# Scatters without batch waits, a reordered first and last batch, and a shorter tail in an mLSTM and mixture-of-experts block

## The reference

```python
xn = layernorm(x)                                # over the 128 features
# s: attention of 4 heads of 32 features, per batch
q, k, v = headwise products of xn with 4x4 blocks of wq, wk, wv
ig, fg  = three times xn through wi, wf, plus bi, bf
log_D   = cumulative log_sigmoid(fg), lower triangle, plus ig
D       = exp(log_D - row_max(log_D))
C       = (q @ k.T / sqrt(32)) * D
h       = (C / (max(|row_sum(C)|, exp(-row_max)) + 1e-8)) @ v
s       = layernorm(h, per head) * (1 + ln_w)
# g: mixture of 8 experts, each token goes to one
top1 = argmax(softmax(xn @ router_w + router_b))
for i in range(8):
    a, b = split(xn @ w1[i] + b1[i])             # 512 and 512
    y = (a * sigmoid(b)) @ w2[i] + b2[i]         # kept for tokens with top1 == i
g = silu(y of the token's expert)
out = x + s * g
```

## Time and profile before

| | us |
|---|---|
| time, median of 3 (range) | 235.09 (234.85 to 235.75) |
| the profiled execution's own time | 235.47 |
| its span, first to last instruction | 233.7 |
| PE busy | 217.2 |
| DVE busy | 162.4 |
| ACT busy | 140.3 |
| POOL busy | 92.6 |

### The profile page before, as it was taken

One profiled execution on the slowest core, in us unless ns is written; L12 is line 12 of the kernel. 1 busy time (PEld: TensorE's weight loads), 2 busy tenths in 40 slices (PEclk: granted clock), 3 DMA queues, 4 the chain that ended last, 5 costly groups with the idle time before them and its releaser, 6 DMA issues.

```text
span 233.7 us, 6082 instructions
## 1 busy us (share of the span) xinstructions
PE 217.2 (93%) x1824; PEld 173.1 (74%) x1834; DVE 162.4 (69%) x491; ACT 140.3 (60%) x326; POOL 92.6 (40%) x130
## 2 busy tenths in 40 slices
PE   8998989678899889999999999999999999998994
PEld 6787654234545454569999999999999999996541
DVE  5998699507467658755877987798779967963170
ACT  2398758456767676877556655665566555552044
POOL 5667930756566563000333333333433333335100
PEclk9999999976999999999999999999999999999999
DMA  6999999930179111400077021011101001000498
GB/s 180 328 363 418 337 205 210 209 111 34 49 202 327 35 48 44 129 3 28 18 223 255 14 67 57 23 57 56 47 28 52 22 26 35 17 22 13 110 341 267
DMA packets 23617, 29.26 MB, mean 125 GB/s; under 512 B 3319, under 2 KB 18687, under 8 KB 23585
## 3 DMA queue, kind: packets, MB, share of 16 engines
q1 hardware_dynamic: 18994, 20.42, 26.5%
q0 software_dynamic: 3424, 8.36, 14.5%
q10 hardware_dynamic: 1168, 0.10, 0.4%
HBM read 19.99 MB, written 9.34 MB: 126 GB/s over the span
## 4 chain that ended last, share of the span: by engine, by line
PE 73%; DVE 13%; issue 5%; ACT 2%; another core or an unknown queue 2%; DMA 2%; POOL 0%; DVEq 0%; SPq 0%; ACTq 0%
PE bank L1213 15%; PE bank L1222 15%; PE head_bank L1213 15%; PE head_bank L1171 5%; PE bank L1183 4%; DVE cm L876 4%; PE bank L1161 3%; DVE stats L711 2%; PE bank L1199 2%; PE head_bank L1141 2%; PE bank L1285 2%; DMA x_sb<-in_L_attn_x 2%; PE bank L1288 1%; PE head_bank L1285 1%
## 5 line engine op out<-in xcount | busy, mean ns | idle before, releaser
L450 POOL DMA_INDIRECT y_tokens<-ffn,idx x39 | 38.6, 991 | 88.1 <-DVE ffn L1004 87.5
L876 DVE TENSOR_TENSOR cm<-dm,head_bank 128x1024 f32<-128x1024 f32 (+1 forms) x32 | 29.1, 951 | 23.7 <-PE head_bank L1171 8.5
L444 POOL DMA_INDIRECT xs_sorted<-xn,pos x32 | 31.1, 973 | 28.0 <-PE head_bank L1171 10.5
L1222 PE MATMUL bank<-w_sb,dm 128*128 x312 | 41.3, 275 | 0.1
L1213 PE MATMUL bank<-xsT,wc 128*128 128x128 f32 x320 | 39.0, 275 | 0.0
L1222 PEld LDWEIGHTS bank<-w_sb,dm 128*128 128x128 f32 x312 | 38.0, 192 | 0.3 <-issue 0.3
L1213 PEld LDWEIGHTS bank<-xsT,wc 128*128 128x128 f32 x320 | 37.3, 192 | 0.0
L1213 PE MATMUL head_bank<-xsT,wc 128*128 128x128 f32 x304 | 37.0, 275 | 0.0
L1213 PEld LDWEIGHTS head_bank<-xsT,wc 128*128 128x128 f32 x304 | 35.5, 192 | 0.0
L586 ACT ACTIVATE wc<-w_sb 128x512 f32 x39 | 24.6, 630 | 14.4 <-issue 14.3
L565 ACT ACTIVATE dm<-bank 128x512 f32<-128x512 f32 x48 | 27.0, 597 | 8.1 <-PE bank L1161 7.5
(11 more groups left out here) (192 smaller groups left out, 345.5 us busy)
## 6 DMA issues: line engine op xcount, KB each, us to landing
x_sb<-in_L_attn_x SPq DMA_DIRECT2D x16, 256.0 KB, 5.1
w_sb<-in_L_ffn_w SPq DMA_DIRECT2D x8, 512.0 KB, 8.9
w_sb<-negated_rows POOLq DMA_DIRECT2D x8, 508.0 KB
xs_sb<-xs_sorted SPq DMA_DIRECT2D x13, 192.0 KB
xs_sorted<-b_sb SPq DMA_DIRECT2D x1, 2048.0 KB, 11.1
w_sb<-y_tokens SPq DMA_DIRECT2D x8, 256.0 KB, 4.4
out_x<-w_sb SPq DMA_DIRECT2D x8, 256.0 KB, 2.5
y_tokens<-ffn,idx POOLq DMA_INDIRECT x39, 2.3
```

Source lines behind the costliest of these rows:

```text
L444: pool.indirect_dma_start(xs_dram, bass.IndirectOffsetOnAxis(ap=pos[:, t:t + 1], axis=0), xn[:, t, :], None).then_inc(s_scat, 16)
L450: pool.indirect_dma_start(y_dram, bass.IndirectOffsetOnAxis(ap=idx[:, j:j + 1], axis=0), ys_sb[:, j // CH % 2, j % CH, :], None, bounds_ch ...
L876: dve.tensor_tensor(cm[:, b % 2, :, m0:m1, :], dm[:, b % 2, :, m0:m1, :], head_bank[:, :, m0 * P:m1 * P].rearrange("p h (m t) -> p h m t", ...
L1222: last = pe.matmul(bank[6 + j % 2][:, 0:D], uT[:, j % 2, c, :], w2_sb[:, bass.ds(e * (HC * D) + c * D, D)], start=(c == 0), stop=(c == HC ...
```

## The change

- GpSimd: the table `SCAT_AT` and the waits for it are gone. The scatters are issued one after the other once `pos` is there.
- VectorE, batch 0: the first step of `positions()` stays ahead; the other steps and the rows of decay 2 stand behind the weighing of batch 0.
- Batch 14: its token rows (TensorE) stand behind the hidden layer of block 0 in iteration 15, and their copy (ScalarE) behind the gate of block 0.
- Last blocks: ScalarE takes the output's sigmoid ahead of the gate for j = 38. VectorE does the silu ahead of the product and the bias for j = 38 and of the bias for j = 39.
- TensorE, tail: the warming before the last x-addition is gone.

```diff
@@ -55,7 +55,6 @@
     TP = T // NPC
     NSTEPS = 25
     SQUARES_AT = {1: (0, 1), 8: (2,), 9: (3,), 16: (4,), 17: (5,), 24: (6,), 25: (7,)}
-    SCAT_AT = [t * 13 // T for t in range(T)]
     GT = 8
     EPS_LN = 1e-5
     EPS_N = 1e-8
@@ -439,8 +438,6 @@
             pool.wait_ge(s_fill, 32)
             pool.wait_ge(s_pos, 1)
             for t in range(T):
-                if SCAT_AT[t] != (SCAT_AT[t - 1] if t else 0):
-                    pool.wait_ge(s_sc, SCAT_AT[t])
                 pool.indirect_dma_start(xs_dram, bass.IndirectOffsetOnAxis(ap=pos[:, t:t + 1], axis=0),
                                         xn[:, t, :], None).then_inc(s_scat, 16)
 
@@ -614,6 +611,12 @@
                 act.activation(sg[:, j % 2, :, :].rearrange("p c t -> p (c t)"), bank[2 * (j % 2) + 1][:, :],
                                ACT.Sigmoid).then_inc(s_th, 1)
 
+            def sigmoid(j):
+                act.wait_ge(s_yb, j + 1)
+                if j >= 2:
+                    act.wait_ge(s_ye, j - 1)
+                act.activation(sy[:, j % 2, :], yb[:, j % 2, :], ACT.Sigmoid).then_inc(s_sy, 1)
+
             decay(0, 0)
             decay(0, 1)
             evac_q(6)
@@ -628,6 +631,7 @@
                 if b == B - 1:
                     act.wait_ge(s_cm, 2 * (B - 1))
                     gate(0)
+                    outputs(b - 1)
                 if b + 2 < B:
                     decay(b + 2, 0)
                 if b == B - 2:
@@ -636,7 +640,7 @@
                 if b + 2 < B:
                     decay(b + 2, 1)
                     decay(b + 2, 2)
-                if b + 1 < B:
+                if b + 2 < B:
                     outputs(b)
                 if b == 5:
                     act.wait_ge(s_seld, 1)
@@ -659,15 +663,14 @@
                     evac_xs(j + 1)
                 if 2 <= j < NBLK - 1:
                     copy_w(j + 1)
+                if j == NBLK - 1:
+                    sigmoid(j - 2)
                 if 1 <= j < NBLK:
                     gate(j)
                 if j == 1:
                     outputs(B - 1)
-                if j >= 2:
-                    act.wait_ge(s_yb, j - 1)
-                    if j >= 4:
-                        act.wait_ge(s_ye, j - 3)
-                    act.activation(sy[:, j % 2, :], yb[:, j % 2, :], ACT.Sigmoid).then_inc(s_sy, 1)
+                if j >= 2 and j != NBLK - 1:
+                    sigmoid(j - 2)
                 for i in SQUARES_AT.get(j, ()):
                     squares(i)
 
@@ -889,12 +892,15 @@
 
             def attention():
                 blocks = experts_of_blocks()
-                for place in positions():
-                    link(place)
+                places = positions()
+                link(next(places))
                 dve.tensor_scalar(left[:, 1, :], sel[:, 0, :], lmask[:, 0, 1:2], lmask[:, 1, 1:2], ALU.mult, ALU.add).then_inc(s_lf1, 1)
-                left_rows(2)
                 for b in range(B):
                     weigh(b)
+                    if b == 0:
+                        for place in places:
+                            link(place)
+                        left_rows(2)
                     if b == 0:
                         dve.wait_ge(s_sel, 2)
                         dve.wait_ge(s_seld, 1)
@@ -1016,6 +1022,8 @@
                     if j >= 2:
                         copy_w(j + 1)
                         step(normals)
+                if j >= NBLK - 1:
+                    silu(j - 2)
                 if 1 <= j < NBLK:
                     product(j)
                     if j == 1:
@@ -1026,7 +1034,7 @@
                     token_index(j // CH)
                 if 1 <= j <= NBLK:
                     add_bias(j - 1)
-                if j >= 2:
+                if 2 <= j < NBLK - 1:
                     silu(j - 2)
                     step(normals)
             while step(normals):
@@ -1245,6 +1253,7 @@
                     pe.wait_ge(s_xone, 1)
                     pe.wait_ge(s_dm, 3 * B)
                     hidden(0)
+                    token_rows(b - 1)
                 if b + 2 < B:
                     log_decay(b + 2, 0)
                 if b == B - 2:
@@ -1280,8 +1289,6 @@
             pe.wait_ge(s_xr, 16 * NPC)
             pe.wait_ge(s_yb, NBLK)
             for g in range(NPC):
-                if g == NPC - 1:
-                    keep_warm(6, g)
                 pe.matmul(bank[g][:, :], ident[:, :], x_sb[:, g * TP:(g + 1) * TP, :], start=True, stop=False)
             for g in range(NPC):
                 pe.wait_ge(s_prod, g + 1)
```

## The result

| | before | after |
|---|---|---|
| time, median of 4 (range) | 235.42 (234.85 to 237.16) | 261.27 (259.74 to 262.58) |
| the profiled execution's own time | 235.47 | 261.54 |
| its span | 233.7 | 259.7 |
| mean granted clock of TensorE | 0.985 | 0.921 |
| weighing of batch 15 starts | 101.02 | 127.83 |

The ratio is 1.1082, with a 95% interval of 1.0996 to 1.1168. The forecast was 239.0 with a range of 232 to 247. Its sign was right; its size was off by 22 us, and the time lies outside the range.

The account below looks back on a forecast made before the run. The prediction took the kernel as bound nearly always by TensorE working or being kept from working. +6.2 - 0.5 - 1.6 = +4.1 on 235.47 gave 239.6, 239.2 as a median, rounded to 239; range 232 to 247.

Parts of the forecast that it names:

- The mechanism: Attention batches: while scatters go back to back, what waits on TensorE is released late, later the longer the stream is.
- only a third scatter costs: Rival, attention batches: a third scatter costs, stream length adds nothing; 235.6 us, or 232.7 at 4.65 throughout; chance 0.25.
- the stream costs nothing: Rival, attention batches: a continuous stream costs nothing after batch 2, batches at 3.2 us; 225.8 us; chance 0.15.
- the pace P: Time per attention batch inside the unpaced scatter stream: taken as 6.07 us, batch 15 weighed 6.2 us later; chance 0.45.
- as bad as its worst batch: Rival, attention batches: pace near 8.84 us beside the stream; 246.3 us, up to 249; chance 0.15.
- a fall of the clock: Part of the worst-pace rival: TensorE's granted clock falls once more, some 3 us, bringing 246.3 up to 249.
- The last batch: Batch 14's token rows moved behind the first expert block's hidden layer fill a TensorE idle: -0.5 us, between 0 and -0.5.
- The last silus: End of expert stage: earlier silus let the last scatter start at 215.3 instead of 216.23, -0.95 us for the reloads.
- The tail as a whole: Last silus and removed warming together: -1.95 us by the rows, taken as -1.6, between -1.0 and -1.95.
- The Trainium skill's rule: Attention batches: engines never wait on anyone, engine and DMA ports cannot contend; stream would cost nothing; prediction said trace disagrees.

Follow-up runs that it names:

- e2_nowait: The kernel before with only the scatters' batch waits removed, held-up series: 261.39 us, ratio 1.1117.
- e1_waits: The changed kernel with the scatters' batch waits put back, quiet series: 221.26 us, ratio 0.9911.
- h2_small: The kernel before with only the edits of last batch, last silus and warming, quiet series: 222.08 us, ratio 0.9943.
- r1_after: The changed kernel again, unaltered, in a second, held-up series: 261.82 us, ratio 1.1130.
- r3_waits: The changed kernel with the scatters' batch waits put back, run again in a held-up series: 237.73 us, ratio 1.0118.
- g2_narrow: The changed kernel with back-to-back scatters moving only 32 of 128 columns, held-up series: 262.49 us, one execution.
- g1_close: The changed kernel with a 96-column memset ahead of each scatter, starts 1.44 us apart, no batch waits, held-up series: 249.02 us, ratio 1.0584.
- f2: The changed kernel with a GpSimd memset ahead of each scatter, starts 1.58 us apart, no batch waits, held-up series: 231.98 us, one execution.
- f3: The changed kernel with plain, unsorted DMAs from GpSimd's queue in place of the 32 indirect scatters, held-up series: 222.91 us, one execution.
- e6: The changed kernel with plain, unsorted DMAs from SP's queue in place of the 32 indirect scatters, held-up series: 220.99 us, one execution.
- r2_before: The kernel before once more, for its trace in the second, held-up series: 237.84 us, one execution.
- f1_two: The changed kernel with waits allowing two scatters per batch, held-up series: 238.48 us, ratio 1.0124.

## Why the prediction was wrong in size

**The mechanism was read rightly, for the held-up kind.** While scatters are issued back to back, what waits on TensorE is released late, and later the longer the stream is. This came true. The scatters run 1.27 us apart from 42.60 to 82.17, as forecast (42.4 to 81.8). With the waits removed from before and nothing else, the loss is there. The rival in which only a third scatter costs (232.7 to 235.6) fell with e2_nowait, and the one in which the stream costs nothing (225.8) with it. In a quiet series that last one is what happens: e1_waits and h2_small have the dense stream and batches of 3.2 us. No row of the kernel before could show that there are two kinds, and the sign came out right because the result was taken in the kind in which the prediction's trace was.

**The step that failed is the pace P.** The text put it as "it can't be below 3.20 and the worst seen is 8.84", took 6.07, and gave +6.2 us. Measured is 127.83 - 101.02 = +26.8. The stream's passage from batch 1 to its end was to be 6.7 batches; it was less than two. The 6.07 was the mean of two unlike batches, 3.30 us (40.09 to 43.39, while the first scatters went out) and 8.84; after has 3.45 and 8.63 there, and then the stop. Both 6.07 and 8.84 were used as a pace that 32 scatters would hold. But the earlier trace rows had releases 3.47 (44.32 to 47.79) and 2.63 us behind the result after a few scatters, where the earlier trace rows had 1.31 after three. The text says "later the longer the stream is" and then bounds by the worst of the shortest stream. A delay that grows with the stream has no upper bound in a burst of eight; the bound was the whole stream: no batch passes until it ends. That is batch 1 at 83.8 and 14 batches at 3.20 behind it, 128.6 for batch 15. The measured 127.83 lies beside it, and so do r1_after (128.8 by this rule, 128.45 measured) and e2_nowait (127.0, 126.68). This rule was made after the result, and it fits in part by luck: batch 2 did pass, at 51.26, the release came 5.8 us behind the last scatter instead of 2.0, and the twelve behind it took 39.84 us, 3.32 each. The rival "as bad as its worst batch" (246 to 249) had the same flaw. Its upper end counts 3 us for a fall of the clock, for which it shows no row; the two batches at and behind the lower level took 1.5 us more in sum than at 3.20 each (3.81 and 4.08). The rival of the third scatter rests on six alternating intervals from batch 5 on; the three before them, from 52.23 to 64.36, take 3.87, 4.41 and 3.85 us and fit neither of its two paces.

**What the delay follows.** From the last scatter of a burst to the release behind it: 1.9 us after three (67.08 to 68.99), and 5.8 after 32 (82.17 to 87.97). In between lie 2.5 after the eight of before (49.69 to 52.23) and 2.7 after the ten of r3_waits (55.61 to 58.28); the other streams of 32 at 1.27 us have 5.6 (r1_after, g2_narrow) and 6.9 (e2_nowait). The plain reading is a backlog: each indirect scatter leaves behind it something that takes longer than 1.27 us, and hand-offs wait for it. The spacing series bears this out in part: at 1.58 us batches take 3.92 us in the mean, and at 1.44 7.8. But a backlog alone would be small at 1.44, and g1_close has its release only 1.8 us after its last scatter (87.79 to 89.56) and yet batches of 7.4 to 10.8 us. So, in a held-up series, the spacing decides, shown by f2, g1 and after; the bytes don't, shown by g2; indirect DMAs to scattered rows do it and plain ones to rows in order don't, shown by f3 and e6 beside after. What the thing is that piles up stays open, and no row names it. Open too is what makes a series held up, without which the same stream costs nothing.

**The clock** followed and did not lead. The granted clock is 1.00 up to 51.26 and 0.50 (the lower level, 1.2 GHz) in the long batch behind it; TensorE had by then been idle since 48.15, the end of its last matmul ahead of the stop. TensorE is busy for 7.87 of 36.73 us there, so by an estimate from that the lower level adds at most some 4 us to what it does, and most of that is hidden inside the stop. The stretch after it is granted 0.95.

**The last batch.** Predicted -0.5; from the weighing of batch 15 to the last second product it is 111.56 instead of 112.23, -0.67. The mechanism is right and the gain a little over the stated bound of -0.5. It is steady: the traces with this edit whose expert stage doesn't wait for its rows have 111.55 to 111.57, those without it (before, r2_before, e2_nowait) 112.2.

**The last silus.** Predicted -0.95, measured from the last second product's end to the last scatter's start, 2.98 (216.23 - 213.25) before and 2.58 after: -0.40. The text let the silus of 37 and 38 end "as now". It had not counted what stands behind the moved silu on VectorE. The timeline after shows it:

```profile
238.93 0.31 ACT L618 ACTIVATE ffn<-ffn 128x128 f32<-128x128 f32 x1 [1.88 <-DVE ffn L1002]
239.34 0.29 DVE L1010 TENSOR_TENSOR ffn<-ffn 128x128 f32<-128x128 f32 x1 [0.45 <-DVE ffn L1002]
240.17 0.29 DVE L1002 TENSOR_TENSOR ffn<-bank,b_sb 128x128 f32<-128x128 f32 x1 [0.54 <-issue]
...
240.61 1.95 PE L1292 MATMUL bank<-x_sb,ident 128*128 128x512 f32 x4 [1.22 <-DVE ffn L1002]
...
241.97 0.98 POOL L447 DMA_INDIRECT y_tokens<-ffn,idx  x1 [0.59 <-issue]
```

The last product ends at 239.39. The bias of block 38 (L1002) stands behind the silu of block 37 (L1010), which waits for its sigmoid, and starts at 240.17, 0.78 after it; before it was 0.19 (213.44 - 213.25). The 0.59 go on to the last silu, the last scatter and the x-additions, which start 1.22 us after the product instead of 0.63. The 2.58 stands, to within 0.02, in every trace with this edit and one scatter per block.

**The tail as a whole** was to give -1.6 and gave -0.10 in the profiled execution (17.13 instead of 17.23). In other kernels with this tail it is between 15.9 and 16.9 (r3_waits 15.91, r1_after 16.31, e1_waits 16.40, h2_small 16.54, f2_spaced 16.94), and 17.23 in e2_nowait and r2_before, which have the tail of before. So the term is -0.1 to -1.3, and the -1.6 was too large: 0.55 of it is the late bias, and the rest varies from run to run with the reloads' landing. In after the third product waits 1.86 us for its piece, in before 0.81. After has its first product at 247.12, 5.15 us after the last scatter's start; before it was 5.07.

**The sum** on the profiled executions closes: +26.8 - 0.67 - 0.10 = +26.0, where 261.54 - 235.47 = 26.07. The three stretches lie end to end, so this says only that no other part of the span moved.

**The Trainium skill's rule** (SBUF — State Buffer, "SBUF: two separate sides"), that TensorE and ScalarE never wait on anyone and engine ports and DMA ports cannot contend, would give no cost. In a quiet series the traces agree, 3.20 us a batch. In a held-up one there is a cost, 36.73 us for a batch with DMA engines 0.13 busy. But the traces show late releases and no wait for a port, so they refute the conclusion that was drawn from the rule, not the rule on ports itself; the prediction's sentence that the trace does not agree with it says more than the earlier trace rows show.

## What to carry to other kernels

A wait that costs its own engine 10 us may be the pacing that keeps the others running: before removing one, ask what the unpaced stream does to its neighbours, and look for a dose that grows faster than in proportion (in before two in a batch cost 0.03 us, three 1.45, the batch beside the first eight 5.64). Such a dose holds only in the pattern in which it was read: with two in every batch, f1_two, the price was 0.5. And measure in more than one series: the same dense stream cost 26 us in one kind and nothing in the other. Where the delay grows with the length of the stream, don't bound it by the worst of the short ones; price also the case that nothing passes until the stream ends. When an instruction is moved ahead on an in-order engine, list what now stands behind it: a silu that waits for its sigmoid held the next block's bias for 0.59 us.

## What the runs showed of the hardware

- In held-up series, indirect DMAs issued by GpSimd 1.27 us apart stopped TensorE, ScalarE and VectorE almost wholly for some 30 us (36.73, 38.11 and 36.63 us for one batch); 1.44 apart, batches took 7.4 to 10.8 us; 1.58 apart, 3.2 to 4.65. Single matmuls for which the profile shows no releaser came 2.1 to 2.8 us apart.
- In quiet series the same 32, 1.27 us apart, delayed nothing (e1_waits, h2_small: batches of 3.2 us).
- Plain DMAs of the same tiles from the same engine, 0.53 us apart, delayed nothing in a held-up series either (222.91 where the kernel before took 236.67).
- The same kernel took 223 us in two series and 235 to 237 in the others, with GpSimd's scatters equally long (0.97 us, 0.30 between). The 12 us lie in the batches: from batch 1 to batch 15 it takes 57.63 us in before and 45.37 in h2_small, which has the same waits and positions. One and the same chip was of both kinds in different series. The held-up traces miss many records of semaphore changes (3128 in before, 3719 in h2_small). What sets the kind is open.
